# A pre-norm block with attention between two ternary feed-forward layers: output product and second feed-forward layer of a tile placed in pieces between the next tile's score and maximum products

## What is computed

```python
x = L0_attn_x                                            # (4, 1024, 512) float32
x = x + 0.5 * ffn(layernorm(x), w_gate_up, w_proj)
x = x + attn(layernorm(x), Wq, bq, Wk, bk, Wv, bv, Wo, bo)
x = x + 0.5 * ffn(layernorm(x), w_gate_up, w_proj)

# attn: 32 query heads, 8 key heads, 16 columns a head, rotary embedding, no mask
scores = jnp.einsum('bhqd,bhkd->bhqk', Q, K) / np.sqrt(HD).astype(np.float32)
w = jax.nn.softmax(scores, axis=-1)
attn = jnp.einsum('bhqk,bhkd->bhqd', w, V)
out = attn.transpose(0, 2, 1, 3).reshape(b, t, D)
return out @ Wo.T + bo

# ffn: weights made ternary in groups of 64, hidden width 2048
gate, up = jnp.split(gu, 2, axis=-1)
h = jax.nn.silu(gate) * up
hn = rms_norm(h)
return jnp.einsum('bsh,dh->bsd', hn, wq_p)
```

## Time and profile before

| | us |
|---|---|
| median of 3 runs (3255.53 to 3263.45) | 3256.95 |
| time of the profiled execution | 3253.83 |
| its span (first to last instruction) | 3252.1 |
| before attention starts on DVE | 1107 |
| the two maximum rounds ahead of the first score | 40 |
| attention | 1261 |
| output product | 129 |
| second feed-forward layer | 715 |

### The profile page before, as it was taken

One profiled execution on the slowest core, in us unless ns is written; L12 is line 12 of the kernel. 1 busy time (PEld: TensorE's weight loads), 2 busy tenths in 40 slices (PEclk: granted clock), 3 DMA queues, 4 the chain that ended last, 5 costly groups with the idle time before them and its releaser, 6 DMA issues. The chain is left out here.

```text
span 3252.1 us, 52798 instructions
## 1 busy us (share of the span) xinstructions
PE 2989.7 (92%) x16038; PEld 1130.8 (35%) x16038; DVE 1981.9 (61%) x2380; ACT 1689.0 (52%) x3156; POOL 890.8 (27%) x756
## 2 busy tenths in 40 slices
PE   1179999999999799999999999999989899999999
PEld 0134444444466322222222222222223344444444
DVE  9943222222277799999999999999922322222221
ACT  4433333333211078888888888888840233333332
POOL 6834444444444200000000000000013344444444
PEclk9999999999999789999999999999999999999999
DMA  3301111110133201111111111111227211110001
GB/s 99 111 27 39 40 39 39 39 39 20 44 96 99 68 22 30 28 28 31 31 30 31 29 28 30 30 29 28 80 78 256 80 40 40 40 39 33 20 26 39
DMA packets 163776, 160.52 MB, mean 49 GB/s; under 512 B 62553, under 2 KB 100697, under 8 KB 163681
## 3 DMA queue, kind: packets, MB, share of 16 engines
q1 hardware_dynamic: 163680, 159.23, 16.5%
HBM read 111.41 MB, written 47.19 MB: 49 GB/s over the span
## 5 line engine op out<-in xcount | busy, mean ns | idle before, releaser
L1270 DVE TENSOR_REDUCE at_neg_max<-at_max_ps 128x1 f32<-128x1024 f32 x1024 | 1206.4, 1220 | 20.7 <-PE at_max_ps L1156 2.4
L1258 ACT ACTIVATE at_probs<-at_score_ps 128x512 f32<-128x512 f32 x2048 | 1057.8, 605 | 166.0 <-PE at_score_ps L1176 165.9
L480 DVE SCALAR_TENSOR_TENSOR f_h<-f_up_ps,hr_factor,f_gate 128x512 f32<-128x512 f32 x256 | 192.2, 751 | 943.8 <-ACT f_gate L572 938.5
L1156 PE MATMUL at_max_ps<-at_km,at_q 48*128 48x512 f16 x2048 | 705.3, 392 | 13.8 <-PEq L749 8.1
L1176 PE MATMUL at_score_ps<-at_q,at_ks 50*128 50x512 f16 x2048 | 623.6, 383 | 37.4 <-ACT at_probs L1258 22.2
L1183 PE MATMUL at_out_ps<-at_probs,at_v 128*32 128x512 f32 x4096 | 546.8, 606 | 0.1
L572 ACT ACTIVATE f_gate<-f_gate_ps 128x512 f32<-128x512 f32 x256 | 152.8, 597 | 708.7 <-PE f_up_ps L645 708.7
L594 POOL TENSOR_TENSOR f_h_lo<-f_h,f_h_hi 128x512 f16<-128x512 f32 x256 | 296.8, 1159 | 761.0 <-ACT f_h_hi L561 761.0
L1452 POOL TENSOR_TENSOR rows<-rows,bias 128x512 f32<-128x512 f32 x32 | 39.4, 1264 | 1397.9 <-ACTq L1391 1313.2
L645 PE MATMUL f_gate_ps<-f_xt_hi,wt 128*128 128x512 f16 x1024 | 389.3, 380 | 20.6 <-ACT f_gate L572 13.8
L659 PE MATMUL f_out_ps<-wt,f_h_hi 128*128 128x512 bf16 x1024 | 388.1, 379 | 3.3 <-POOL f_h_lo L594 3.3
(11 more groups left out here) (101 smaller groups left out, 2294.3 us busy)
## 6 DMA issues: line engine op xcount, KB each, us to landing
rows<-x SPq DMA_DIRECT2D x40, 1024.0 KB, 5.7
x<-rows SPq DMA_DIRECT2D x16, 1024.0 KB, 4.5
tw_raw<-units SPq DMA_DIRECT2D x48, 256.0 KB, 2.6
at_q<-qk_parts SPq DMA_DIRECT2D x384, 32.0 KB, 1.8
rows<-x SPq DMA_DIRECT2D x32, 256.0 KB, 2.9
at_q<-at_max_parts SPq DMA_DIRECT2D x512, 1.0 KB
att<-at_out SPq DMA_DIRECT2D x256, 32.0 KB
ao_a<-att SPq DMA_DIRECT2D x8, 1024.0 KB
```

The source lines that it names most:

```text
L480: nc.vector.scalar_tensor_tensor(out=h[:, c % HB, :], in0=up_ps[:], scalar=hidden_range.factor, in1=gate[:, c % 2, :], op0=ALU.mult, op1=A ...
L1156: done = nc.tensor.matmul(max_ps[u % 2][:, half * QB:(half + 1) * QB], q[k][rows, j // SLOTS, h * QB + c * P:h * QB + (c + 1) * P], km[k][ ...
L1258: nc.scalar.activation(probs[:, kc % PBUF, j, :], score_ps[pos % RING][:], ACT.Exp, scale=HD ** -0.5).then_inc(exps, 1)
L1270: nc.vector.tensor_reduce(neg_max[:, h, column:column + 1], max_ps[u % 2][:], AX.X, ALU.max, negate=True).then_inc(maxed, 1)
```

## The change

Attention now runs tile by tile: 64 rounds again (`NR`), in the order batch, half of the queries, key head, so that 8 rounds (64 steps) give all heads of one tile of 512 queries. The program after the projections is one block, written out without loops over `LAST` = 614 steps. A step does what it did, and after each slot's score and maximum product PE issues a piece of the work on earlier tiles (`Following`; `Place` says which). In a tile's 64 positions `u`: the gate and up products at u = 0 to 31 (two a slot, one chunk in two steps), then from u = 35 four blocks of 7 steps, one for each sub-tile. A block holds the 32 products of the second layer in 22 slots, and for the next tile 4 float32 output products (in slots 1 and 3 of the block's steps 1 and 2), the layer norm and the turning. Steps 0 to 37 of the 614 have attention alone; the first blocks (tile 0's output product) stand at steps 73 to 100; the first gate product is at step 102; the last attention step is 511; the rest have no attention.

The two feed-forward PSUM banks come from the maxima's buffers: there are now two maximum buffers of one bank each, DVE reduces each half alone, and one more instruction a round joins the halves. The second buffer of the queries, keys and probabilities changes too (`KEEP`, `PBUF`). Hidden units of a tile are all kept, so the second layer runs after the first is complete for the tile.

```diff
-QB = 512
+QB = TT
 NB = T // QB
 KC = T // P
-NG = B * HKV
+NR = NTILE * HKV
 MU = GH * QB // P
+MH = T // QB
 MSTEP = MU // KC
 SU = KC * GH
 RING = 3
-PBUF = 4
+PBUF = 2
+KEEP = 4
 TURN_AT = 2
...
+OFF = 38
+TILE = HKV * KC
+BLOCK0 = 35
+BLOCK = 7
+WEIGHT_SLOTS = [(r, i) for r in range(BLOCK) for i in range(GH) if not (r == 0 and i < 2 or r in (1, 2) and i % 2)]
...
+    def __init__(self, step):
+        tau, self.u = divmod(step - OFF, TILE)
+        tau -= 1
+        self.now = tau if 0 <= tau < NTILE else None
+        self.nxt = tau + 1 if 0 <= tau + 1 < NTILE else None
+        block, self.r = divmod(self.u - BLOCK0, BLOCK)
+        self.s = block if 0 <= block < SUB else None
+        self.ended = block - 1 if self.r == 0 and 1 <= block <= SUB else None
+
+
+STEPS = NR * KC
+LAST = OFF + (NTILE + 1) * TILE
...
+    def sync(self, sp, p):
+        t = p.nxt
+        if t is not None:
+            if p.u == TILE - OFF + 1:
+                for stored in self.att_stored:
+                    sp.wait_ge(stored, (t + 1) * (HKV // 2 * OUT_DMAS * 16))
+                sp.dma_start(self.d[:], self.den[t].rearrange("j (s t) -> (j s) t", t=P)).then_inc(self.d_in, 16)
+                after(sp, self.prods, t * SUB)
+                sp.dma_start(self.a[:], self.att[t].rearrange("(c p) t -> p c t", p=P)).then_inc(self.a_in, 16)
+            if p.u == 31:
+                sp.wait_ge(self.recips, t + 1)
+                sp.dma_start(self.inv_den[t].rearrange("j (s t) -> (j s) t", t=P), self.d[:]).then_inc(self.inv_stored, 16)
+                sp.wait_ge(self.inv_stored, t * 16 + 16)
+                after(sp, self.scaled, t * SUB)
+                for c in range(DC):
+                    heads = P // HD
+                    sp.dma_start(self.dn[:, c, :], self.inv_den[t][c * heads:(c + 1) * heads, :].unsqueeze(1).broadcast_to(
+                        [heads, HD, TT])).then_inc(self.a_in, 16)
...
+    def tensor(self, pe, p, i):
+        nc, t, u = self.nc, p.now, p.u
+        if t is not None and u < 2 * HC:
+            c, k = u // 2, u % 2
+            ps = self.up_ps if k else self.gate_ps
+            if i == 0:
+                if c == 0 and k == 0:
+                    pe.wait_ge(self.los, t * SUB + SUB)
+                    after(pe, self.ys, t * SUB)
+                elif k == 0:
+                    pe.wait_ge(self.silus, t * HC + c)
+                elif c >= 1:
+                    pe.wait_ge(self.hs, t * HC + c)
+            for part in (self.xt_hi, self.xt_lo):
+                last = nc.tensor.matmul(ps[:], self.wt[:, 2 * c + k, i, :], part[:, i, :],
+                                        start=(i == 0 and part is self.xt_hi),
+                                        stop=(i == DC - 1 and part is self.xt_lo))
+            if i == DC - 1:
+                last.then_inc(self.ups if k else self.gates, 1)
+        if t is not None and u == BLOCK0 and i == 0:
+            pe.wait_ge(self.accs, t * (HC - 1) + (HC - 1))
+            for s in range(SUB):
...
+        if t is not None and p.s is not None and (p.r, i) in WEIGHT_SLOTS:
+            s, at, n = p.s, WEIGHT_SLOTS.index((p.r, i)), len(WEIGHT_SLOTS)
+            for j in range(at * 2 * HC // n, (at + 1) * 2 * HC // n):
+                c, part = j // 2, (self.h_hi, self.h_lo)[j % 2]
+                if j == 0 and s == 0:
+                    pe.wait_ge(self.hlos, t * HC + HC)
+                elif j == 0:
+                    pe.wait_ge(self.ys, t * SUB + s)
+                last = nc.tensor.matmul(self.out_ps[:], part[:, c, s * P:(s + 1) * P],
+                                        self.wt[:, 2 * HC + (c // DC) * DC:2 * HC + (c // DC) * DC + DC, c % DC, :],
+                                        start=(j == 0), stop=(j == 2 * HC - 1))
+                if j == 2 * HC - 1:
+                    last.then_inc(self.outs, 1)
+        t = p.nxt
+        if t is not None and p.s is not None:
+            s = p.s
+            if p.r in (1, 2) and i % 2:
+                c = (p.r - 1) * 2 + i // 2
+                if c == 0:
...
+                last = nc.tensor.matmul(self.row_ps[:], self.a[:, c, s * P:(s + 1) * P], self.w_o[:, c, :],
...
+            if p.r == 6 and i == 2:
+                pe.wait_ge(self.normed, t * SUB + (s + 1))
+                for c in range(DC):
+                    last = nc.tensor.transpose(self.turn_ps[:, c * P:(c + 1) * P],
+                                               self.xn[:, s, c * P:(c + 1) * P], self.ident)
+                last.then_inc(self.turned, 1)
...
+    def scalar(self, act, p, i):
+        nc, t, u = self.nc, p.now, p.u
+        if t is not None:
+            if u < 2 * HC and u % 2 == 1 and i == 0:
+                c = u // 2
+                act.wait_ge(self.gates, t * HC + (c + 1))
+                after(act, self.hs, t * HC + c)
+                nc.scalar.activation(self.gate[:], self.gate_ps[:], ACT.Silu).then_inc(self.silus, 1)
...
+            if 2 <= u <= 2 * HC and u % 2 == 0 and i == 2:
+                c = u // 2 - 1
...
+                nc.scalar.copy(self.h_hi[:, c, :], self.h[:, c % 2, :]).then_inc(self.hhis, 1)
+            if 3 <= u <= 2 * HC + 1 and u % 2 == 1 and i == 2:
+                c = (u - 3) // 2
...
+                nc.scalar.square(self.sqsum[:] if c == 0 else self.sq[:], self.h[:, c % 2, :]).then_inc(self.sqs, 1)
+        t = p.nxt
+        if t is not None and p.ended is not None and i == 0:
+            s = p.ended
+            act.wait_ge(self.turned, t * SUB + (s + 1))
+            nc.scalar.copy(self.xt_hi[:, :, s * P:(s + 1) * P],
+                           self.turn_ps[:].rearrange("p (c n) -> p c n", n=P)).then_inc(self.his, 1)
...
+            if 2 <= u <= 2 * HC and u % 2 == 0 and i == 0:
...
+                nc.vector.scalar_tensor_tensor(out=self.h[:, c % 2, :], in0=self.up_ps[:], scalar=self.range.factor,
+                                               in1=self.gate[:], op0=ALU.mult, op1=ALU.mult).then_inc(self.hs, 1)
...
+            if p.ended is not None and i == 0:
...
+                nc.vector.scalar_tensor_tensor(out=x[:, s, :], in0=self.out_ps[:], scalar=self.inv[:, s:s + 1],
+                                               in1=x[:, s, :], op0=ALU.mult, op1=ALU.add).then_inc(self.ys, 1)
...
+        if u == 31 and i == 2:
...
+            nc.vector.reciprocal(self.d[:], self.d[:]).then_inc(self.recips, 1)
+        following = 0 if u == 34 else p.s + 1 if p.s is not None and p.r == 6 and p.s + 1 < SUB else None
+        if following is not None and i == 1:
+            s = following
+            if s == 0:
+                dve.wait_ge(self.a_in, (t + 1) * (A_DMAS * 16))
...
+            nc.vector.tensor_tensor(part, part, self.dn[:, :, s * P:(s + 1) * P], ALU.mult).then_inc(self.scaled, 1)
+        if p.ended is not None and i == 2:
...
+            nc.vector.tensor_tensor(self.xt_lo[:, :, part], self.turn_ps[:].rearrange("p (c n) -> p c n", n=P),
+                                    self.xt_hi[:, :, part], ALU.subtract).then_inc(self.los, 1)
...
+        if p.r == 3 and i == 0:
...
+            nc.vector.tensor_tensor(x[:, s, :], x[:, s, :], self.row_ps[:], ALU.add).then_inc(self.added, 1)
+        if p.r == 3 and i == 2:
...
+            nc.vector.bn_stats(self.stats[:], x[:, s, :]).then_inc(self.stat, 1)
...
+        if p.r == 5 and i == 1:
...
+            nc.vector.tensor_scalar(self.xn[:, s, :], x[:, s, :], self.mv[:, s, 0:1], self.rstd[:, s:s + 1],
+                                    ALU.subtract, ALU.mult).then_inc(self.normed, 1)
...
+                at = m * (MU * MH) + u * MH + half
+                after(pe, maxed, at - 1)
+                nc.tensor.matmul(max_ps[half][:], q[m % KEEP][rows, j // SLOTS, c * P:(c + 1) * P],
+                                 k_rows[m % KEEP][rows, half * QB:(half + 1) * QB],
+                                 start=True, stop=True).then_inc(m_done, 1)
...
+            for step in range(LAST):
+                n, kc = divmod(step, KC)
+                place = Place(step)
...
+                        scores(n, kc, i, turned)
+                        if n + 2 < NR:
+                            maxima(n + 2, kc * MSTEP + i // 2, i % 2)
+                    fo.tensor(pe, place, i)
+                if 1 <= step <= STEPS:
+                    weigh((step - 1) // KC, (step - 1) % KC)
...
 
-            def split_maxima(m, h, ps):
+            def join_maxima(m):
+                dve.wait_ge(maxed, (m + 1) * (MU * MH))
+                nc.vector.tensor_tensor(neg_max[:, m % 2, :], neg_half_max[:, m % 2, 0, :], neg_half_max[:, m % 2, 1, :],
+                                        ALU.min).then_inc(joined, 1)
```

More of the change, by code:

```diff
@@ L1024 @@
[L1024 to L1046 removed]
+        self.qk_in = [sem(f"qk_in{k}") for k in range(KEEP)]
@@ L1047, in attention @@
+def attention(nc, data, fo, ident, before):
+    q, k_rows, v = data.q, data.k, data.v
+    qk_in, v_in = data.qk_in, data.v_in
     with ExitStack() as ctx:
@@ L1261, in _, with copy_output @@
```

(37 more changed lines are left out.)

643 lines of the change are left out of this document (292 added, 351 removed).

## The result

The changed kernel takes 3573.43 us (median of 4 runs, 3568.72 to 3582.2) against 3257.11 (3255.53 to 3263.45) for the kernel before: a ratio of 1.097, 95% interval 1.0945 to 1.0996. It is slower by 9.7%. The forecast was 3520 with 3300 to 3640 around it.

The account below looks back on a forecast made before the run. DVE was taken to bound attention, PE the second layer. Terms of 45, 231, 114, 1734, 121 and 165 us made 2410, 265 more than 2145; on 3253.8 that gave 3519, forecast as 3520 us, range 3300 to 3640.

Parts of the forecast that it names:

- The crossings: PE's changes of array division around each piece, nine a step: 0.10 us taken for each, bounds zero and 0.12.
- Free crossings: Rival: no price between half-array and whole-array work on PE; 3305 us, still slower; chance 0.13.
- Gate and up steps: Attention steps with gate or up products (u below 32): 4.65 us each, 149 us for 32 steps.
- Blocks: Four blocks of 7 steps a tile, second-layer and output products among attention: 31 us each, 124 for four.
- The rest of a tile: Four remaining positions at 3.1 each, DVE's 2.1 and 1 to 2 us for spread reciprocals: 16 us.
- The start and attention alone: Two maximum rounds and a first wait, 45 us; then steps 0 to 72 at 3.17 each, 231 us.
- Tile 0's output product: Steps 73 to 101: 29 at 3.17 plus 5.5 us a block, 114 us.
- the last 26 steps: The 26 steps to attention's end, after the six tiles: 121 us.
- the tail: The last tile alone after attention, with its waits, blocks, remaining products and last store: 165 us.
- PE's clock: Rival: PE falls to its low clock in steps with attention alone; 75 us more, 3600 us; chance 0.09.
- Table loads: ACT's loads around each silu, 1.28 us each; rival: each costs 0.6 more, 3650 us, chance 0.05.
- An unbroken stream of PE: Rival: free crossings and no waits for banks, gate or up step 3.5 us; 3120 us, a gain; chance 0.08.

Follow-up runs that it names:

- e5: Changed kernel with the exponential in place of silu and all pieces of a step together behind slot 1: 3366.3 us (1.034).
- e2: Changed kernel with the pieces in twos, behind slots 1 and 3, five changes of division a step in place of nine: 3613.21 us (1.1107).
- e3: Changed kernel with the exponential in place of silu and the pieces in twos behind slots 1 and 3: 3471.94 us (1.0677).
- e4: Changed kernel with four one-bank maximum buffers in the first 11 rounds, two of them the idle feed-forward banks: 3524.42 us (1.0828).
- e9: e8 with the join of the maxima's halves moved behind slot 1 of the next round's first step: 3270.17 us (1.0038).
- e1: Changed kernel with the exponential in place of silu, so no table loads between attention's exponentials: 3509.92 us (1.0775).
- e8: Changed kernel with tanh for silu, pieces behind slot 1, four early maximum buffers, turning in slot 2, reciprocals two steps earlier: 3276.54 us (1.006).

## Why the prediction was right

Direction, mechanism and range held; the sum was 55 us short (2465 after 1107, forecast 2410). Six tiles make 39 of the 55. By its own steps:

- **The crossings.** The direction that no trace of before showed costs 0.10 (0.32 against 0.22), the value taken. Free crossings fell with it. e5 shows the price in time: plain steps 0.49 shorter for five crossings of nine, and 144 us in all, with DVE's added room in it. e2 and e3, where DVE lacked that room, didn't get it.
- **Gate and up steps.** Forecast 4.65, measured 4.79. The mechanism is the forecast's: the even step's first score waits for the odd step's second exponential. The term was mis-sized there: forecast 4.85 for the odd step, measured 5.04 in the one shown and 4.95 in its neighbours. The second exponential is done at 4.90, where I had 4.80 (each hand-off on ACT is 0.02 to 0.03 later), and its release to PE takes up to 0.14, where I had 0.05. The even step took 4.44 against 4.40. And the step ahead of a turning takes 5.78, 0.8 more, which is 0.10 a step, where I had put 0.03 for the copy and the turning together. Two steps took 9.48 in place of 9.25. Over 6.4 tiles of 32 steps, 0.14 is 29 us, more than half of the shortfall.
- **Blocks.** Forecast 31 us, 4.43 a step, measured 4.47 in most tiles and up to 4.56 in one: 1 to 4 us a tile.
- **The rest of a tile.** Forecast 16, measured 15 to 18, the longer ones with more waiting for the spread reciprocals. A tile came to 295.4 (1772.6 / 6) against 289.
- **The start and attention alone.** Forecast 45 and 231 to the end of step 72, 276; measured 281, the value products of step 72 starting at 1387.32 and taking 1.0. The first score came at 1154.34, 2 us late. A plain step took 3.11 and a round 25.3, both as forecast; steps 2 and 3 took 4.73 and 4.20, the clock being at its lower level until 1169. (The window above shows 232.6 / 72 = 3.23 a step, as it holds those two and the 5.7 of step 73.) e4 shows the cause of the 3.1, two buffers in place of four: 49 us.
- **Tile 0's output product, the last 26 steps, the tail.** Forecast 114, 121 and 165; measured 114, 123 and 170. (In the tail the forecast's 17 less 10 is 7, not 6, which changes nothing.)
- **The rivals.** PE's clock stood at half speed in the two maximum rounds and until 1169, and at 1.00 from there to 1390, so attention alone did not lower it. The clock matters elsewhere, in the few microseconds behind a long wait in e2, and in two steps of three tiles in e9. Table loads cost 1.28 and no more: silu starts 0.01 after a load ends (2097.56 + 1.28, 2098.85), no load of the 219 behind 1200 has more than 0.02 before it or 0.01 behind it, and the drain that the Trainium skill (ScalarE: Activation LUTs, What ACT_TABLE_LOAD costs) adds shows nowhere in the trace. An unbroken stream of PE, the gaining side, needed steps under 3.9; even e9, with the loads gone and four crossings, stays at 3.96. That rival was given its 0.08 by a wrong comparison: ACT's 8.5 us for two steps, named as speaking for it, is more than the 2 × 3.5 of PE that it assumes, and 4.25 a step is above 3.9. In the pair shown ACT is busy for 7.99 us, 4.0 a step, so with the loads in place it could not have come true.

What I didn't see until the runs is how far the costs cover each other. e2 and e3 were reckoned from the crossings and the loads, and missed by 133 and 127 us, because DVE's late bank, and in e2 the turning, took over what the crossings gave back.

## What to carry to other kernels

Before work of another shape is put between an engine's instructions, count how often the shape changes and put it in as one piece: nine changes of PE's division a step made it 4.44 us, four made it 3.95 (e1, e5). Ask also what the engines beside it need between bursts. One piece behind the second pair gave DVE time to free both banks, and 144 us; the same products in two pieces didn't, and gave 38 (e3). Count what the filled gap is worth first: here PE idled 0.4 us of a 2.4 us step, which four crossings use up.

## What the runs showed of the hardware

A small DVE instruction with both operands in SBUF was held until POOL's instruction ended. Of the 64 joins of e8 (128x16), 26 ran into an addition on POOL; each of these ended 0.03 us after it and took 0.97 to 1.14 us. The other 38 took 0.17 to 0.18. DVE's reductions from PSUM took 0.67 to 0.69 beside POOL's additions, as long as without them. The Trainium skill, SBUF — State Buffer, Who interferes with whom, says that a DVE instruction with two SBUF inputs contends with a GpSimd instruction that reads SBUF; e8's join agrees, and so does e9, where moving it brought the mean from 547 to 186 ns.
